# Residual quantizer on one Trainium2 core: groups of three score tiles that run across the borders of the streams, and a semaphore of their own for the first constants

## The reference, cut to what matters

```python
def _gn(v, G=32, eps=1e-05):          # 32 groups of 32 channels: mean and variance of each channel of an image
    ...
def _L0_conv_ref(embeddings, codebooks):      # codebooks: 8 stages x 512 codes x 32 channels
    x = embeddings.transpose(0, 2, 3, 1).reshape(-1, e)       # 16384 pixels x 32
    def stage(res, cb):
        d = jnp.sum(res * res, axis=1, keepdims=True) - 2.0 * jnp.einsum('ne,ke->nk', res, cb) + jnp.sum(cb * cb, axis=1)
        idx = jnp.argmin(d, axis=1)
        q = cb[idx]
        return (res - q, q)
    _, qs = jax.lax.scan(stage, x, codebooks)
    quant = jnp.sum(qs, axis=0)
    ...
x = x + _L0_conv_ref(_gn(x), L0_conv_codebooks)
```

## Time and profile before

| | us |
|---|---|
| median of 3 runs | 1776.92 (1776.67 to 1776.98) |
| the profiled execution, its own time | 1778.08 |
| its span | 1776.2 |
| quantizer, first instruction to the next block's first | 0 to 922 |
| period in the steady part | 12.82 |

### The profile page before, as it was taken

One profiled execution on the slowest core, in us unless ns is written; L12 is line 12 of the kernel. 1 busy time (PEld: TensorE's weight loads), 2 busy tenths in 40 slices (PEclk: granted clock), 3 DMA queues, 4 the chain that ended last, 5 costly groups with the idle time before them and its releaser, 6 DMA issues. The chain is left out here.

```text
span 1776.2 us, 35638 instructions
## 1 busy us (share of the span) xinstructions
PE 1483.5 (84%) x10836; PEld 660.6 (37%) x10836; DVE 1248.3 (70%) x4964; ACT 963.2 (54%) x1640; POOL 1075.8 (61%) x780
## 2 busy tenths in 40 slices
PE   1799999989999999999937999857777577877776
PEld 0333333333333333333306777536565322222221
DVE  3899999989998999999943445442221555656586
ACT  1488888878887888888832434210000034444364
POOL 4568998978988789898960322320000355757586
PEclk8699999999999999999968999979999889989898
DMA  6000000000000000000005555000000100000000
GB/s 141 8 2 8 5 8 4 2 12 3 9 4 10 4 2 9 4 2 2 2 17 107 107 107 107 0 18 0 0 0 0 43 0 1 1 1 13 1 13 24
DMA packets 16036, 35.49 MB, mean 20 GB/s; under 512 B 5492, under 2 KB 7128, under 8 KB 15852
## 3 DMA queue, kind: packets, MB, share of 16 engines
q1 hardware_dynamic: 14124, 31.96, 8.0%
q10 hardware_dynamic: 1728, 1.35, 0.3%
HBM read 9.47 MB, written 2.10 MB: 7 GB/s over the span
## 5 line engine op out<-in xcount | busy, mean ns | idle before, releaser
L427 POOL TENSOR_SCALAR l_onehot<-l_ib,c_iota 128x512 bf16<-128x512 f16 x256 | 399.7, 1561 | 42.0 <-ACT l_ib L375 41.2
L521 DVE FIND_INDEX8 l_idx<-l_top,l_scored 128x8 uint32<-128x256 f32 x1024 | 414.1, 422 | 0.0
L247 PE MATMUL ps<-l_ct_slot,l_res 32*128 32x512 f32 x2048 | 408.2, 608 | 0.0
L538 DVE CUSTOM_DVE_ANT_0 l_scored<-ps,l_gain 128x256 f32<-128x256 f32 x1024 | 380.7, 419 | 31.1 <-ACT l_gain L360 29.7
L360 ACT ACTIVATE l_gain<-ps 128x768 f32<-128x768 f32 (+1 forms) x384 | 283.2, 738 | 114.1 <-PE ps L247 114.1
L1534 POOL TENSOR_TENSOR l_isum<-l_term 128x512 f32<-128x512 f32 x160 | 199.0, 1269 | 119.0 <-DVE l_term L1618 78.8
L268 PE MATMUL ps<-l_onehot,l_cbp_slot 128*32 128x512 bf16 x3072 | 217.0, 390 | 7.7 <-POOL l_onehot L427 4.4
L241 PE MATMUL ps<-l_csq,l_row_slot 32*128 32x512 bf16 x1024 | 155.5, 396 | 26.3 <-DVE l_top L538 12.7
L1463 ACT ACTIVATE ps<-ps,l_minus 128x512 f32<-128x512 f32 x192 | 118.2, 663 | 84.7 <-DVE l_term L1624 58.9
L705 PE MATMUL ps<-l_wc,l_xi 100*128 100x192 f32 x768 | 134.8, 333 | 31.1 <-DMA l_xi<-l_xt 31.1
L247 PEld LDWEIGHTS ps<-l_ct_slot,l_res 32*128 32x128 f32 x2048 | 155.9, 194 | 11.6 <-issue 0.9
(11 more groups left out here) (152 smaller groups left out, 2044.4 us busy)
## 6 DMA issues: line engine op xcount, KB each, us to landing
l_xi<-l_xt SPq DMA_DIRECT2D x48, 384.0 KB, 7.1
X<-in_x SPq DMA_DIRECT2D x16, 128.0 KB, 7.8
out<-X SPq DMA_DIRECT2D x16, 128.0 KB, 2.1
l_ct<-in_codes_t SPq DMA_DIRECT2D x4, 448.0 KB, 13.8
l_ct_slot<-l_ct SPq DMA_DIRECT2D x7, 256.0 KB, 2.3
l_cbp_slot<-l_cbp SPq DMA_DIRECT2D x8, 96.0 KB, 1.9
l_wt<-in_l_w SPq DMA_DIRECT2D x1, 768.0 KB, 4.2
l_w_off<-in_l_w_off SPq DMA_DIRECT2D x1, 576.0 KB, 3.3
```

What stands on the lines that cost most here:

```text
L247: pe.matmul(ps[:, at + n - FIRST[k], :], res[rows, i, P * tt:P * (tt + 1)], ct_slot[rows, par, :], start=False, stop=True, skip_group_chec ...
L427: nc.gpsimd.tensor_scalar(onehot[:, i % 2, g, 0, :], ib16[:, i % 2, g, :], iota[:, 0:1], None, ALU.is_equal).then_inc(s_near, 1)
L521: nc.vector.max_index(idx8[:, i % 2, n, :], top[:, i % 2, n:n + 1].to_broadcast([P, 8]), scored[:, WIDE * (k % 3) + n - FIRST[k], :]).then ...
L538: nc.vector.tensor_tensor_reduce(out=scored[:, WIDE * (k % 3) + m, :], in0=ps[:, WIDE * (k % 2) + m, :PAIRED], in1=gain[:, WIDE * (k % 2) ...
```

## The change

Two things, and what they need. First, the 128 tiles of a stage are cut in threes without regard to the streams: 43 groups (the last has 2 tiles). A group belongs to the stream of its first tile, so the periods of a stage have 6, 5, 5, 6, 5, 5, 6 and 5 groups; the other steps keep their slots 0 to 5, and in a period with five groups slot 5 has no scores. Banks and buffers alternate by the group's number in the stage. Second, `csq_w`, `part_mask` and `eps` are loaded first and counted by `s_first`; who needs the other constants waits for `s_in` later. And DVE's work for quarters 1 to 3 is done in between the groups of periods 0 and 1 (`late_quarters`).

```diff
-GROUPS = (3, 3, 3, 3, 2, 2)
-SLOTS = len(GROUPS)
...
+WIDE = 3
+STAGE_TILES = UNITS * TILES
+GROUPS = -(-STAGE_TILES // WIDE)
+END = [min(WIDE * (g + 1), STAGE_TILES) for g in range(GROUPS)]
+OWNED = [[g for g in range(GROUPS) if WIDE * g // TILES == i] for i in range(UNITS)]
+SLOTS = max(len(o) for o in OWNED)
+FIRST_CONSTS = ("part_mask", "eps")
...
+        def slot(w, i, k):
+            if k >= len(OWNED[i]):
+                return None
+            g = OWNED[i][k]
+            return g, (w - i) * TILES, range(WIDE * g, END[g])
...
 # PE
-            pe.wait_ge(s_in, START + 16 * INPUTS)
+            pe.wait_ge(s_first, START + 16 * (1 + len(FIRST_CONSTS)))
...
-                at = WIDE * (k % 2)
+                g, tiles, group = slot(w, i, k)
+                at = WIDE * ((g + par) % 2)
                 if k == 0:
                     pe.wait_ge(s_res, START + w + 1)
-                if k >= 2:
-                    pe.wait_ge(s_top, START + w * TILES + END[k - 2])
...
+                if group[-1] // TILES > i:
+                    pe.wait_ge(s_res, START + w + 2)
+                if g >= 2 or not opening(w, i):
+                    pe.wait_ge(s_top, START + before(tiles, g, 2))
...
             def spread(v, i, g):
+                if isinstance(v, int) and v == 0:
+                    pe.wait_ge(s_in, ready)
...
-                    if scoring:
+                    if scoring and slot(w, i, k):
                         scores(w, i, par, k)
...
 # ACT
-            act.dma_start(csq_w[:], io["csq_w"]).then_inc(s_in, 16)
-            act.dma_start(const["eps"][:], io["eps"]).then_inc(s_in, 16)
+            act.dma_start(csq_w[:], io["csq_w"]).then_inc(s_first, 16)
+            for name in FIRST_CONSTS:
+                act.dma_start(const[name][:], io[name]).then_inc(s_first, 16)
...
+            deviation(0, range(1))
...
-                    if scoring:
-                        at = WIDE * (k % 2)
-                        act.wait_ge(s_score, START + w * TILES + END[k])
...
+                    if scoring and slot(w, i, k):
+                        g, tiles, group = slot(w, i, k)
+                        at = WIDE * ((g + par) % 2)
+                        act.wait_ge(s_score, START + tiles + END[g])
...
+                    if isinstance(w, int) and w == 0 and k == 3:
+                        deviation(1, range(1, J))
+                        act.wait_ge(s_in, START + 16 * (len(CONSTS) - len(FIRST_CONSTS)))
...
 # POOL, ahead of its additions to X
+            pool.wait_ge(s_in, START + 16 * (len(CONSTS) - len(FIRST_CONSTS)))
...
 # DVE
+            def late_quarters(w, k):
+                if w == 0 and k < 3:
+                    measure(1, k + 1)
+                if w == 0 and k == 2:
+                    gather(1, rest)
+                if w == 0 and k == 4:
+                    invert(1, rest)
+                if w == 0 and k == 5:
+                    normalise(1)
+                if w == 1 and k in (1, 4):
+                    normalise(2 if k == 1 else 3)
...
-            statistics(1, rest)
-            normalise(1, rest)
...
+                        if g or not opening(w, i):
+                            dve.wait_ge(s_top, START + before(tiles, g, 1))
+                            dve.sem_inc(s_alone, 1)
+                        if g < 2 and par == 0 and not opening(w, i):
+                            dve.wait_ge(s_found, START + before(tiles, g, 2))
+                            dve.sem_inc(s_alone, 1)
+                        dve.wait_ge(s_gain, START + groups + (g + 1))
...
+                        if g:
+                            find(g - 1, par)
+                        elif not opening(w, i):
+                            find(GROUPS - 1, 1 - par)
...
+                    if isinstance(w, int) and w < 2:
+                        late_quarters(w, k)
                     if k == 3 and mid:
```

More of the change, by code:

```diff
@@ L328, in _ @@
             for name in CONSTS:
-                if name != "eps":
+                if name not in FIRST_CONSTS:
                     act.dma_start(const[name][:], io[name]).then_inc(s_in, 16)
@@ L514, in _, with scored_at @@
             nc.vector.tensor_copy(csq[:], csq_left[:]).then_inc(s_csq, 1)
-            statistics(1, rest)
-            normalise(1, rest)
[L518 to L524, removed]
+            def scored_at(g, par):
+                return WIDE * ((g + GROUPS * par) % 3)
@@ L525, in period, with find @@
+            def find(g, par):
+                for m, n in enumerate(range(WIDE * g, END[g])):
+                    u = n // TILES % 2
+                    nc.vector.max_index(idx8[:, u, n % TILES, :],
+                                        top[:, u, n % TILES:n % TILES + 1].to_broadcast([P, 8]),
+                                        scored[:, scored_at(g, par) + m, :]).then_inc(s_found, 1)
+            def period(w, i, scoring, par, use, groups):
                 early, mid = (back(w, i, par, n) for n in (1, 3))
@@ L542, in period @@
-                    if k == 0 and early:
-                        find(early[1], SLOTS - 1)
-                    if k and scoring:
-                        find(i, k - 1)
+                    if scoring and slot(w, i, k):
+                        g, tiles, group = slot(w, i, k)
+                        at = WIDE * ((g + par) % 2)
+                        if g or not opening(w, i):
[5 more added lines that the diff above has]
+                        dve.wait_ge(s_gain, START + groups + (g + 1))
+                        dve.sem_inc(s_alone, 1)
+                        for m, n in enumerate(group):
+                            nc.vector.tensor_tensor_reduce(
+                                out=scored[:, scored_at(g, par) + m, :], in0=ps[:, at + m, :PAIRED],
+                                in1=gain[:, at + m, :], scale=1.0, scalar=LOWEST, op0=ALU.add, op1=ALU.max,
+                                accum_out=top[:, n // TILES % 2, n % TILES:n % TILES + 1]).then_inc(s_top, 1)
+                        if g:
+                            find(g - 1, par)
+                        elif not opening(w, i):
+                            find(GROUPS - 1, 1 - par)
@@ L546, in period @@
+                    if k == 0 and not scoring and i == 0:
+                        dve.wait_ge(s_top, START + ALL * TILES)
+                        dve.sem_inc(s_alone, 1)
+                        find(GROUPS - 1, 1)
+                    if isinstance(w, int) and w < 2:
+                        late_quarters(w, k)
                     if k == 3 and mid:
```

90 lines of the change are left out of this document (39 added, 51 removed).

## The result

The changed kernel takes **1835.0 us** (median of 4 runs, 1832.8 to 1835.9), against 1776.95 for the kernel before: ratio 1.032, 95% interval 1.031 to 1.034. It was forecast slower, at 1851 us, 1788 to 1888. The profiled execution took 1835.9, with a span of 1834.1, 57.9 us more than before.

A forecast was written before the change was run, and what follows sets the result against it. DVE and PE were taken as nearly full, with a 4.21 us chain from line 549 to slot 0 causing DVE's wait. 1778.1 + 32 (waits) + 52 (clock) - 10 (start) = 1852, as a median 1851 us; range 1788 to 1888.

The forecast's parts named there:

- What bounds the kernel: Steady periods of 12.82 us: DVE and PE nearly full, DVE waiting 0.27 us for ACT's gain ahead of slot 0.
- The chain of 4.21 us: Line 549 through PE's sum and scores and ACT's gain to DVE's next slot 0; no score work can shorten it.
- DVE: DVE's own work in a period: same maxima and finds, 13.90 us with six groups and no wait.
- The stall: DVE waits 1.41 us ahead of slot 0 in five of eight periods, making them 13.09 us; +32 us in all.
- the waits on `s_found`: DVE's waits for its own finds, long done by then; claimed to cost nothing.
- PE's holes: PE idles about 1.2 us ahead of spread(3) and 0.55 us ahead of line 316 in five-group periods.
- The clock: PE's granted clock falls behind idle time at 37 five-group borders, 1.4 us each: +52 us.
- The row at 100.42: Profile row of the kernel before: after a single wait of 0.96 us, PE's scores ran at 1.2 GHz.
- The start: Before the steady periods: constants loaded first, quarters' work moved between groups, POOL later; -10 us, ends -6 and -13.
- POOL's 11 us in hand: POOL's slack of 11.14 us before its first one-hot, all used by its later begin.
- The clock holds: Rival: PE keeps full clock despite short idle times; 1799 us, chance 0.17.
- DVE alone sets the pace: Rival, at the border: waits vanish and each period costs DVE's 12.42 us; 1743 us, chance 0.13.

The follow-up runs named there:

- fifth: Changed kernel with groups cut by stream again (48 a stage) and DVE's addition of the middle to the residual ahead of slot 3's maxima; 1770.5 us.
- seventh experiment: Changed kernel with groups cut by stream as 3, 3, 3, 3, 3, 1 (48 a stage); 1769.8 us.
- second experiment: Changed kernel with six more matmuls on PE in each slot 5 that has no scores; 1799.3 us.
- fourth experiment: Changed kernel with DVE's addition of the middle to the residual ahead of slot 3's maxima, not behind its finds; 1760.7 us.

## Why the prediction was right, and where it was off

- **What bounds the kernel: half right.** The chain of 4.21 us from line 549 to the next slot 0 stayed 4.21 in the changed kernel and with the empty slot 4. What I missed is the second arm through slot 1: in the kernel before it is this arm that sets 12.82 us, and the one that I named would give 12.70. In a five-group period the arm through slot 0 is the longer one, 13.09, so the miss did not touch this forecast; it spoilt the fifth and seventh experiments.
- **DVE**: a six-group period was forecast at 13.90 and took 13.89.
- **The stall: right.** 13.09 forecast; 13.08 to 13.22 measured in 15 of 35 periods as they stand, and in 33 of 35 once the clock was kept up. Worth +34.6 if every one takes 13.09, where I had +32, with 0.39 a stage off for a find that the last group lacks. With the clock up (second experiment) the interval that lacks it took 12.83 or 12.82, some 0.26 less, where a stage begins without a wait for `s_found`, and 13.16 where one is there. So the saving was partly real, and the waits on `s_found`, which I had put at nothing, ate it at every second stage.
- **PE's holes: right** in place and roughly in size. Forecast were 1.2 and 0.55 us; measured at the 37 borders 1.13 and 0.87 (15 times), 0.87 and 1.13 (7), 1.13 and 0.38 to 0.52 (10), 1.13 and 0.25 (5).
- **The clock: mechanism right, the term mis-sized.** I had 37 falls of 1.4 us, +52. There were 20 in the 35 periods outside the loop's turns, at 39.2/20 = 2.0 us each: +39. So the forecast had too many falls and too low a price for one, and the two errors partly cancelled. The price counted slot 0's scores and pick and left out line 336, which in 17 of the 20 ran partly or wholly at the lower clock as well (up to 2.05 us in place of 1.10). The holes are shorter in the period behind a long one (the second 0.25 to 0.52 us and not 0.87), and so a long period is often followed by one of 13.09. Filling the holes returned 35.7 us. The row at 100.42, on which I had put more weight than on the closing table of the Trainium skill, "TensorE: Matmul & The Clock Gate", pointed the right way: that table asks for no idle gaps of some 3 us; outside the loop's turns the longest of these holes was 1.13 us, and the clock fell 20 times. The same page of the Trainium skill has the section "A second HAM failure mode: psum-queue depth-cycling", which speaks of short idling between groups of matmuls; the rows from 257.88 to 260.43 agree with it.
- **The start: right**, -10.0 for -10, and POOL's 11 us in hand were used up as said. The split between semaphore and quarters stays open.
- What is left is the loop's turns, 4 us cheaper than before for no cause that I looked for, and 2 us at the end. In sum 13 us of the 16 between 1851 and 1835 are the clock's term.
- **The rivals.** "The clock holds" was given 1799, and that kernel, made by filling the holes, took 1799.3. "DVE alone sets the pace" was given 1743 with the point at a stall below 0.64 us a border; the empty slot 3, which takes the stall away, took 1745.1.

## What to carry to other kernels

When groups of work are made fewer on an engine that looks full, look for a ring of waits through the other engines and count what the waiting engine still has to do beside it at every place: leaving out a group can cost more there than it saves. If a slot has to stay empty, its place is a free choice; put it where the work on both sides still covers the longest chain, here worth 90 us with no other edit. And short idle times on TensorE are priced with the clock behind them, not by their own length.

## What the runs showed that I had not expected

- In the changed kernel TensorE fell to 1.2 GHz behind 20 of the 22 pairs of holes of 1.13 and 0.87 us (in either order), behind 2 of the 10 of 1.13 and 0.38 to 0.52 us (at 342.65 and 800.11, each time in the period behind a larger pair that it had stood), and behind none of the 5 of 1.13 and 0.25. Behind a single hole of 1.13 us it held in all 30 cases of the fourth experiment; with the empty slot 4 a hole of 1.63 us made it fall 18 times of 22, one of 1.3 once in 11. In the kernel before it had fallen behind a single 0.96. So longer idle time makes the fall more frequent, but the same holes need not do the same, and no bound can be read from these runs.
- Six matmuls whose result nobody reads made the kernel 36 us faster.
- PE's scores cost 1.18 us for three tiles, two, or one: in the seventh experiment too, the slot with one tile takes PE as long as that with three.
